# Queries and output projection of four heads of 96 packed into three tiles of 128

## The reference, cut to what matters

```python
hidden = concat([context, latents], axis=1)            # 64 + 256 rows
q = (latents @ Wq.T).reshape(b, q_len, 16, 96)         # four heads to a group
k = (hidden @ Wk.T).reshape(b, s_len, 4, 96)
v = (hidden @ Wv.T).reshape(b, s_len, 4, 96)
attn = softmax(einsum('bkgqd,bksd->bkgqs', q, k) / sqrt(96))
out = einsum('bkgqs,bksd->bkgqd', attn, v)             # back to 16 x 96 = 1536
return out @ Wo.T
```

## Time and profile before

| what | us |
|---|---|
| median of three runs | 1833.43 (1831.36 to 1834.33) |
| the profiled execution, its own time | 1829.38 |
| its span, first to last instruction | 1827.6 |
| PE busy in the span | 1475.9 (81%) |
| DVE busy in the span | 1129.2 (62%) |
| ACT busy in the span | 464.1 (25%) |
| mean granted clock of TensorE | 0.871 of full |

### The profile page before, as it was taken

One profiled execution on the slowest core, in us unless ns is written; L12 is line 12 of the kernel. 1 busy time (PEld: TensorE's weight loads), 2 busy tenths in 40 slices (PEclk: granted clock), 3 DMA queues, 4 the chain that ended last, 5 costly groups with the idle time before them and its releaser, 6 DMA issues.

```text
span 1827.6 us, 19239 instructions
## 1 busy us (share of the span) xinstructions
PE 1475.9 (81%) x6585; PEld 1165.1 (64%) x6585; DVE 1129.2 (62%) x2623; ACT 464.1 (25%) x994; POOL 311.6 (17%) x186
## 2 busy tenths in 40 slices
PE   4549989989899898979837877858997676679998
PEld 3426666667676666757626766747886565468786
DVE  2466667656776666846796757554458588864241
ACT  2213334232342323313222202112212222222020
POOL 2201111011121111202011102113432312012020
PEclk9779999999899989999955689559998878789999
DMA  4341222213222211122101112100111100001011
GB/s 127 121 127 55 72 66 73 76 45 90 60 69 71 79 48 58 53 74 61 35 24 41 41 38 70 44 16 13 55 49 46 35 1 0 1 23 58 12 37 46
DMA packets 99362, 96.43 MB, mean 53 GB/s; under 512 B 13090, under 2 KB 72370, under 8 KB 99266
## 3 DMA queue, kind: packets, MB, share of 16 engines
q1 hardware_dynamic: 98754, 94.35, 17.8%
q0 software_dynamic: 512, 0.85, 0.2%
HBM read 84.34 MB, written 10.82 MB: 52 GB/s over the span
## 4 chain that ended last, share of the span: by engine, by line
PE 32%; DVE 19%; issue 2%; ACT 1%; DVEq 0%; ACTq 0%
PE bank L1643 29%; DVE st L1128 1%; DVE xn L1146 1%; DVE mx L1496 1%; DVE e L1510 1%; DVE nf_y L1587 1%; DVE xT L1107 1%; DVE sm L1508 1%; PE bank L1983 1%; PE bank L1939 1%; DVE e L1499 1%; PE bank L1668 1%; DVE eT L1516 1%; DVE rt L1117 0%; DVE rt L1116 0%
## 5 line engine op out<-in xcount | busy, mean ns | idle before, releaser
L1643 PE MATMUL bank<-xT,slots 128*128 128x512 f32 (+1 forms) x1920 | 466.9, 401 | 8.8 <-DVE xT L1107 6.8
L802 POOL TENSOR_TENSOR slots<-staging,slots 128x1024 fp32r<-128x1024 f32 (+4 forms) x97 | 229.3, 2367 | 1189.0 <-ACT slots L890 1188.9
L1643 PEld LDWEIGHTS bank<-xT,slots 128*128 128x128 f32 (+1 forms) x1920 | 355.6, 186 | 105.3 <-DVE xT L1107 5.4
L1983 PE MATMUL bank<-nf_y,nf_d 128*128 128x512 f32 (+2 forms) x495 | 193.3, 450 | 82.9 <-DVE nf_w L1597 53.5
L1587 DVE TENSOR_SCALAR nf_y<-nf_w 128x512 fp32r<-128x512 f32 (+2 forms) x495 | 225.0, 483 | 19.4 <-PE bank L1983 18.2
L1643 PE MATMUL bank<-slots,h 128*128 128x512 f32 (+1 forms) x728 | 181.6, 409 | 21.0 <-DVE h L1235 14.9
L1983 PEld LDWEIGHTS bank<-nf_y,nf_d 128*128 128x128 f32 (+1 forms) x495 | 97.0, 201 | 137.9 <-DVE nf_y L1587 63.3
L1643 PEld LDWEIGHTS bank<-slots,h 128*128 128x128 f32 (+1 forms) x728 | 142.2, 196 | 58.0 <-DVE h L1235 15.7
L890 ACT ACTIVATE slots<-staging 128x1024 fp32r<-128x1024 f32 (+4 forms) x97 | 98.1, 1018 | 203.4 <-PE bank L1643 184.1
L1107 DVE TENSOR_TENSOR q<-bank,q 96x256 fp32r<-96x256 f32 (+3 forms) x120 | 61.0, 508 | 125.7 <-ACT q L880 125.7
L1201 DVE TENSOR_TENSOR x<-bank,x 128x512 f32<-128x512 f32 x72 | 49.8, 692 | 140.9 <-PE bank L1643 140.7
(11 more groups left out here) (244 smaller groups left out, 1944.1 us busy)
## 6 DMA issues: line engine op xcount, KB each, us to landing
staging<-in_L_wqkT SPq DMA_DIRECT2D x16, 480.0 KB, 3.5
nf_out<-nf_w SPq DMA_DIRECT2D x30, 256.0 KB, 2.1
staging<-nf_out SPq DMA_DIRECT2D x30, 256.0 KB, 2.9
staging<-in_L_woT SPq DMA_DIRECT2D x16, 384.0 KB, 3.5
staging<-in_L_w SPq DMA_DIRECT2D x12, 512.0 KB, 3.9
nf_a<-nf_max SPq DMA_DIRECT2D x40, 128.0 KB, 3.4
nf_r<-nf_rcp SPq DMA_DIRECT2D x40, 128.0 KB, 3.3
nf_w<-in_L_w SPq DMA_DIRECT2D x15, 256.0 KB, 3.4
```

The source lines that it names most:

```text
L802: g.tensor_tensor(lo, split_source(i), hi.bitcast(FP32), ALU.subtract).then_inc(*sig.mark("weight_low", i))
L1643: ins = mm(dst, l_, r_, start=i == 0, stop=i == len(passes) - 1)
L1983: mm(banks[NF_BANK][0:rows, 0:size], nf_d[0:rows, j - 1, 0:rows], nf_y[0:rows, i % STAIR_RING, 0:size], start=j == 1, stop=j == NPART).the ...
```

## The change

Three tiles of 128 rows take the place of four heads of 96. Tile j holds the 96 rows of head j (0 to 2) and, in partitions 96 to 127, 32 rows of head 3 (`spare(j)`: rows 32j to 32j + 31 of it). The host lays the rows of `Wq` and the columns of `Wo` out in this order.

- `q0_` runs three times for a stage, each into 128 partitions. ACT evicts two pieces: partitions 0 to 95 to their old place, and partitions 96 to 127 to partitions 32j to 32j + 31 of head 3's place, so that head 3 is whole in 96 partitions for the scores. DVE evicts the low parts of both pieces.
- `pv0` of heads 0 to 2 is evicted as before. That of head 3 is evicted in three pieces of 32 rows x 256, each from partitions 32j up to partitions 96 to 127 of tile j, on ACT and on DVE.
- `o0` contracts three tiles of 128 rows instead of four of 96.
- The signals of ACT and DVE are given behind the last piece. `schedule` has three `q0` a stage, one each at j = 5, 6 and 7. The chunks of `Wo` are 128 x 1024 and 128 x 512.

```diff
-    steps += [("k0", 0), ("kc0", 0)] + [("q0", 0, h) for h in range(HPG)]
+    steps += [("k0", 0), ("kc0", 0)] + [("q0", 0, j) for j in range(QT0)]
...
-                steps += [("q0", s + 1, h) for h in ((0, 1), (2,), (3,))[j - 5]]
+                steps.append(("q0", s + 1, j - 5))
...
-        q0 = sb("q0", [HD0, 2, 2, HPG, HALF], F32R, s0)
+        q0 = sb("q0", [P, 2, 2, HPG, HALF], F32R, s0)
...
-            for i in range(2):
-                rows = a["L0_woT"][(s % G0 * HPG + 2 * i) * HD0:(s % G0 * HPG + 2 * i + 2) * HD0]
-                chunk(("o0", s, i), HD0, (2, D), [((slice(None),), rows.rearrange("(h p) n -> p h n", p=HD0))])
+            for i, n in enumerate((2, 1)):
+                rows = a["L0_woT"][(s % G0 * QT0 + 2 * i) * P:(s % G0 * QT0 + 2 * i + n) * P]
+                chunk(("o0", s, i), P, (n, D), [((slice(None),), rows.rearrange("(h p) n -> p h n", p=P))])
...
-                high("q0", (s, h), q0[:, s % 2, 0, h], psum(("q0", s, h))[0:HD0])
+                act.wait_ge(*sig.when("q0_product", (s, j)))
+                sc.activation(q0[0:HD0, s % 2, 0, j], bank[0:HD0], ACT.Copy)
+                sc.activation(q0[spare(j), s % 2, 0, QT0], bank[HD0:P], ACT.Copy).then_inc(*sig.mark("q0_high", (s, j)))
...
+                act.wait_ge(*sig.when("pv0_product", n))
+                for j in range(QT0):
+                    ins = sc.activation(q0[HD0:P, s % 2, 0, j, cs], bank[spare(j), 0:S], ACT.Copy)
+                ins.then_inc(*sig.mark("pv0_high", n))
...
-                low("q0", (s, h), q0[:, s % 2, 1, h], psum(("q0", s, h))[0:HD0], q0[:, s % 2, 0, h])
+                dve.wait_ge(*sig.when("q0_high", (s, j)))
+                v.tensor_tensor(q0[0:HD0, s % 2, 1, j], bank[0:HD0], q0[0:HD0, s % 2, 0, j].bitcast(FP32), ALU.subtract)
+                low("q0", (s, j), q0[spare(j), s % 2, 1, QT0], bank[HD0:P], q0[spare(j), s % 2, 0, QT0])
...
+                for j in range(QT0):
+                    ins = v.tensor_tensor(q0[HD0:P, s % 2, 1, j, cs], bank[spare(j), 0:S],
+                                          q0[HD0:P, s % 2, 0, j, cs].bitcast(FP32), ALU.subtract)
...
-                qk(s, ("q0_product", (s, h)), h * HD0, (h + 1) * HD0, lambda k: xt(k, hf * HALF, (hf + 1) * HALF), bank[0:HD0])
+                qk(s, ("q0_product", (s, j)), j * P, (j + 1) * P, lambda k: xt(k, hf * HALF, (hf + 1) * HALF), bank[:])
...
-                pe.wait_ge(*sig.when("q0_low", (s, h)))
+                pe.wait_ge(*sig.when("q0_low", (s, min(h, QT0 - 1))))
...
-                pairs = [([q0[:, s % 2, p, h, i * P:(i + 1) * P] for p in range(2)], [w[h // 2][p][:, h % 2] for p in range(2)])
-                         for h in range(HPG)]
+                pairs = [([q0[:, s % 2, p, j, i * P:(i + 1) * P] for p in range(2)], [w[j // 2][p][:, j % 2] for p in range(2)])
+                         for j in range(QT0)]
```

More of the change, by code:

```diff
@@ L24 @@
 HPG = H0 // G0
+QT0, SPARE0 = HPG * HD0 // P, P - HD0
 KEYS0 = S + CTX
@@ L94, with spare @@
 NF_BANK = 7
+def spare(j):
+    return slice(j * SPARE0, (j + 1) * SPARE0)
 def fwidth(f):
@@ L913, in kc0_, with q0_ @@
                 high("kc0", s, k0[:, s % 2, 0, :, S:], psum(("kc0", s))[0:HD0, 0:BPH * CTX].rearrange("p (b n) -> p b n", b=BPH))
-            def q0_(s, h):
-                high("q0", (s, h), q0[:, s % 2, 0, h], psum(("q0", s, h))[0:HD0])
+            def q0_(s, j):
+                bank = psum(("q0", s, j))
+                act.wait_ge(*sig.when("q0_product", (s, j)))
+                sc.activation(q0[0:HD0, s % 2, 0, j], bank[0:HD0], ACT.Copy)
+                sc.activation(q0[spare(j), s % 2, 0, QT0], bank[HD0:P], ACT.Copy).then_inc(*sig.mark("q0_high", (s, j)))
             def scores0(n, s, bl, h):
@@ L936, in pv0 @@
             def pv0(n, s, bl, h):
-                high("pv0", n, q0[:, s % 2, 0, h, bl * S:(bl + 1) * S], psum(("pv0", n))[0:HD0, 0:S])
+                cs, bank = slice(bl * S, (bl + 1) * S), psum(("pv0", n))
+                if h < QT0:
+                    high("pv0", n, q0[0:HD0, s % 2, 0, h, cs], bank[0:HD0, 0:S])
+                    return
+                act.wait_ge(*sig.when("pv0_product", n))
+                for j in range(QT0):
+                    ins = sc.activation(q0[HD0:P, s % 2, 0, j, cs], bank[spare(j), 0:S], ACT.Copy)
+                ins.then_inc(*sig.mark("pv0_high", n))
             def up0(f, hf):
@@ L1192, in pv0 @@
             def pv0(n, s, bl, h):
-                cs = slice(bl * S, (bl + 1) * S)
-                low("pv0", n, q0[:, s % 2, 1, h, cs], psum(("pv0", n))[0:HD0, 0:S], q0[:, s % 2, 0, h, cs])
+                cs, bank = slice(bl * S, (bl + 1) * S), psum(("pv0", n))
+                if h < QT0:
+                    low("pv0", n, q0[0:HD0, s % 2, 1, h, cs], bank[0:HD0, 0:S], q0[0:HD0, s % 2, 0, h, cs])
+                    return
+                dve.wait_ge(*sig.when("pv0_high", n))
+                for j in range(QT0):
+                    ins = v.tensor_tensor(q0[HD0:P, s % 2, 1, j, cs], bank[spare(j), 0:S],
+                                          q0[HD0:P, s % 2, 0, j, cs].bitcast(FP32), ALU.subtract)
+                ins.then_inc(*sig.mark("pv0_low", n))
             def add_to_x(stage, key, t, src, name=None, mark=None, scale=None):
@@ L1714, in scores0 @@
                     bank = claim(("scores0", n, i), ("exp0", (n, i)))
-                    l_ = [q0[:, s % 2, p, h, bl * S + i * P:bl * S + (i + 1) * P] for p in range(2)]
+                    l_ = [q0[0:HD0, s % 2, p, h, bl * S + i * P:bl * S + (i + 1) * P] for p in range(2)]
                     product(bank[:, 0:KEYS0], [(l_, [k0[:, s % 2, p, bl] for p in range(2)])])\
@@ L2024, in lay_out @@
     rows = [((c * HPC + h) // REP3) * HD3 + j for c in range(KT) for h in range(HPC) for j in range(HD3)]
+    tiles = np.array([[h * HD0 + d for d in range(HD0)] + [QT0 * HD0 + h * SPARE0 + d for d in range(SPARE0)]
+                      for h in range(QT0)]).reshape(-1)
+    heads = np.concatenate([g * HPG * HD0 + tiles for g in range(G0)])
     return {
@@ L2028, in lay_out @@
         "ctxT": t(d["ctx_4096"].reshape(B * CTX, D).T),
-        "L0_wqkT": t(np.stack([np.concatenate([wq[g * HPG * HD0:(g + 1) * HPG * HD0], wk[g * HD0:(g + 1) * HD0]]).T
+        "L0_wqkT": t(np.stack([np.concatenate([wq[g * HPG * HD0 + tiles], wk[g * HD0:(g + 1) * HD0]]).T
                                for g in range(G0)])),
         "L0_wvT": t(d["L0_xattn_Wv"].T),
-        "L0_woT": t(d["L0_xattn_Wo"].T),
+        "L0_woT": t(d["L0_xattn_Wo"].T[heads]),
         "L0_wgT": t(d["L0_ffn_w_gate"].T), "L0_wuT": t(d["L0_ffn_w_up"].T), "L0_wdT": t(d["L0_ffn_w_down"].T),
```

7 lines of the change are left out of this document (4 added, 3 removed).

## The result

| kernel | median us | ratio to before | 95% interval |
|---|---|---|---|
| before | 1832.39 (1831.10 to 1834.33) | | |
| changed | 1861.84 (1853.28 to 1864.55) | 1.0152 | 1.0115 to 1.0188 |

Each median is that of four runs; for the kernel before, that is one run more than in the table ahead of the prediction. The change makes the kernel 29 us slower. I had forecast 23 us faster, with 0.87 for faster; the time lies above the range. The profiled execution of the changed kernel has a span of 1862.8 us, 35.2 more than before. That is 6 us more than the medians differ: the profiled execution before took 1829.38 us, 3 less than its median, and the one after 1864.55, 3 more than its own. What follows divides up these 35.2 us.

What follows compares the result with a forecast made beforehand. PE was taken as the bound, DVE as runner-up. Savings of 42.1 us, less 7.7, 5.6 and 7.7 for added waits, plus 2 for weights, gave 23 us: 1810.4 us, range 1800 to 1822, chance 0.58.

Steps and rivals of the forecast that it cites:

- What bounds the kernel: Attention 0, 140 to 675 us: PE is the bound, waiting 47 us, nearly all for DVE, the runner-up.
- What PE loses: Query and output products over eight stages: 180 counted matmuls less at 0.234 us, 42.1 us saved at full clock.
- rival (B): Longer stalls bring five more windows of lowered PE clock, costing 17 us: 1827 us, chance 0.14.
- What ACT and DVE gain: Added eviction pieces in attention: 24 us more DVE work and 22 more ACT work in all, covered on average.
- The ends of stages: Behind the last query product at seven stage ends, the second piece lengthens PE's stall by 1.1 us each: 7.7 us.
- The value products of head 3: Extra pieces at j = 1 cost 0.7 us in each of eight stages, 5.6 us; j = 2 is covered.
- The bank's eviction: Mid-stage waits for the dequantisation bank: PE arrives earlier, half its lead is lost, 11 x 0.7 = 7.7 us.
- Weights: The halved second chunk of Wo takes POOL 1.74 instead of 2.44 us, eight times; 2 us gained.
- The background moves: Six of 495 dequantisation parts move from attention 0 to later steps; 1.4 us saved and spent, net nothing.
- (C): DVE's chain decides at every meeting point, once PE's waits exceed some 89 us: slower, 1843 us, chance 0.08.

Runs made afterwards that it cites:

- The lag of 4 on the kernel before: Kernel before, with PE's matmul of a dequantised part four parts behind DVE instead of two, nothing else: 1796.3 us, 0.9807.
- Late low parts: Changed kernel with DVE's two low parts of the queries one step later in its order, same instructions: 1828.2 us, 0.9971.
- The output half alone: Kernel before with only the output projection packed, head 3's value product evicted in three shifted pieces, queries as before: 1831.0 us, 0.9992.
- the kept room: Changed kernel with the planner giving the query step at j = 5 the room of two products, so no background part moves: 1861.6 us, 1.0151.
- the run with the filled idle time: Changed kernel with PE computing the second score tile four times more in 18 units behind a query product: 1859.6 us, 1.0146.
- the one with the second piece alone: Kernel before, all matmuls kept, with a second piece of 32 rows in each of its 32 query evictions: 1871.6 us, 1.0221.

## Why the prediction was wrong, point by point

**What bounds the kernel.** That PE had work for all but 47 us was right, and so was that nearly all waits are for DVE. The conclusion was wrong. I read DVE's 98.7 us of waits for ACT's high parts as lateness of PE passed on, hence as slack. They are waits inside a chain on which PE depends at the other end: PE waits only 7.7 us for parts, but in 14 places, in nine of them by 0.15 to 0.17 us. At such a place the two arrive together, and what is added to DVE's side goes to PE in full, as the two places around 370 and 360 us show. The lag of 4 on the kernel before, worth 35 us with no work saved, shows how tightly the two engines were coupled.

**What PE loses** was right at full clock: 0.234 us for each of the matmuls, nine of them for an output product (185.87 to 187.97, 2.10 us), full tiles for the price of narrower ones. But the sum had no term for the clock, which appears only as rival (B); the slower work took 21.4 us back.

```profile
185.87 2.26 PE L1669 MATMUL bank<-slots,q 128*128 128x512 f32 x9
187.97 0.63 PE L2009 MATMUL bank<-nf_y,nf_d 128*128 128x512 f32 x2
```

**What ACT and DVE gain**: the durations were right to the hundredth, with no price for the shift. What the pieces lose is the overlap. For three value pieces I had priced 0.27 us for each added one on ACT and 0.34 on DVE, and they took 0.38 and 0.43; a query's second piece lengthens the chain by 0.60 on ACT and 0.71 on DVE, where I had 0.5 and 0.6. "As averages, DVE then has 52.5 us of work in a stage where PE has 61. That is cover enough for the mean" was true and beside the point. Late low parts with the same average ran 34 us faster.

**The ends of stages** is the step that failed. 1.1 us was set for a query's second piece, at seven ends, 7.7 us in all. It was 1.3 us (1.6 with ACT's later start), and it can reach PE behind each of 21 products: behind 14 of them the waits for parts grew, by some 24 us. The small waits of 0.15 us behind query products in the middle of stages stood in the timeline before; I looked only where PE already stalled by whole microseconds.

**The value products of head 3**: 5.6 us taken, with j = 2 as "covered". The output half alone shows more: of 22 us none arrives with the pieces in place, and 11 with them late. So their price is some 22 us where I had 5.6, the clock included, and half of it hangs on their place in DVE's order.

**The bank's eviction** had 7.7 us, and the waits rose by some 5 us. This was about right in size. **Weights**: POOL took 1.35 us for a halved chunk; what it gave back can't be told apart.

**The background moves**, taken at nothing: right for the kernel's time, by the kept room, though each of the two stretches shifts by 6 to 7 us.

**Rivals.** (C) named the right side and something of the mechanism, DVE's chain deciding, at the wrong places: it had the largest part for the bank's eviction, and nothing for query products in the middle of a stage. Its condition was waits of PE beyond some 89 us, the old waits and the 42 saved; they are 91 in a window in which they were 49. By waits alone this only breaks even. (B), a falling clock, happened as well, at 21 us, and this makes the kernel slower. I had treated (B) and (C) as alternatives, with 0.14 and 0.08, but the waits bring the clock down, as the run with the filled idle time and the one with the second piece alone show, so they come together: any price set for idle time of PE had to be set higher for this.

**What stays open**: how much of the loss is POOL's low part of a weight chunk, which lengthens a part by 1.7 us at three of the 14 places, runs beside DVE at some of the others too, and was not taken away in any run; how the clock's fall divides between the two halves of the change; and what holds the packed queries back at lag 4, where the waits for DVE's background are still 21 us above the old form's.

## What to carry to other kernels

When an engine that isn't the bound gets longer steps, don't ask for its share of busy time but for what the bounding engine takes from it next: follow its order from the lengthened step to the next signal, and set that against the work that the other has in hand. Repeated waits of 0.15 us for the same releaser were no small matter here but a sign that there was no slack. Before saving work on the bounding engine it can pay more to loosen the coupling: one figure for the lag gave 35 us here, with no work saved. The best kernel of this study, at 1785.6 us, has that figure and only the output half of the change. That half puts pieces into 2 of 8 units of a stage and leaves the evictions behind the query products as they were.

## What the runs showed of the hardware

- An eviction of 32 partitions to other partitions than it reads takes as long as one of 96 in place, on ACT and on DVE (0.374 and 0.420 us for 256 columns, 0.592 and 0.694 for 512). Such pieces don't overlap with their neighbours: for 256 columns 0.435 us from start to start instead of 0.33 on DVE, 0.38 instead of 0.27 on ACT.
- While POOL computes the low part of a weight chunk, a background part on DVE can take up to 2.6 us instead of 0.42 (2.13 at 558.64 after; the longest is 2.60 before and 2.58 after).
- 32 us of extra matmuls in PE's waits cost nothing (1859.6 against 1861.8), and the granted clock of the stretch went from 0.91 to 0.94. The same 2361 or 2362 matmuls took 503.1 us of busy time at 0.96 and 520.2 at 0.92, where only evictions had been added.
